# Sixteen-head attention in a four-layer kernel: value products with the probabilities as stationary side

## The chip, the cores and the metric

The kernel runs on one core of a Trainium2 chip. The metric is the device time of one execution in microseconds (us). The engines are named as in the profile: PE is TensorE's matmul, PEld its load of the stationary operand, DVE is VectorE, ACT ScalarE, POOL GpSimd, SP SyncE.

## The reference

The program has four layers. Each adds a cross attention between 512 positions of x (four batches, width 128) and a context of 77 positions, and then a mixture of experts. The change touches the attentions of layers 0, 1 and 2, which have 16 heads of 8 dimensions. Layer 0's, cut:

```python
q = split_heads(queries @ Wq + bq)      # (b, 16, 512, 8)
k = split_heads(keys @ Wk + bk)         # (b, 16, 77, 8)
v = split_heads(values @ Wv + bv)
scores = jnp.einsum('bhqd,bhkd->bhqk', q, k) / jnp.sqrt(jnp.float32(HD))
scores = jnp.where(mask, jnp.float32(-1000000000000000.0), scores)
attn = jax.nn.softmax(scores, axis=-1)
ctx = jnp.einsum('bhqk,bhkd->bhqd', attn, v)
ctx = ctx.transpose(0, 2, 1, 3).reshape(b, sq, d)
return ctx @ Wo + bo
```

Layers 1 and 2 are alike with another mask; layer 1 has no output projection. Layer 3's attention has 8 heads of 128 dimensions and other code. Everything is in float32.

## The kernel before

The three sixteen-head attentions are called stages 0, 1 and 2 here (`attention(l)` in the code). Each is followed by its experts (`feed`). Every engine runs its own program; they meet at semaphores.

A stage goes through four batches of 512 queries. The 16 heads are split into two halves of 8 (index p). The 8 x 77 = 616 rows (head, key) of a half are cut into five pieces of up to 128 rows (`PIECES`), so there are 40 units u a stage (4 batches, 2 halves, 5 pieces), 120 in all. The order is a list of numbered slots n, written out by hand in `attention_plan`: in slot n each engine does the items of that slot, in the order of its own loop, and the PE's loop also does `turned(n - 8)` and `values(n - 10)`. Slot numbers below are counted within a batch, modulo 10.

For each unit, PE forms the scores with (head, key) on the partitions and 512 queries as columns (`turned`: a mask product in bf16, L2198, and a key product, L2200 to L2203); ACT takes the exponential into one of four buffers `pT` (L1190); PE then multiplies by the values (`values`, L2219). The value operand `vx` is block-shaped: for a row of head h it holds the 8 values of that head and a 1 in the head's 9 columns (VC = 9), zeros in the other heads' columns, 72 columns for 8 heads. It is the stationary side; the 512 queries of `pT` move. The five pieces of a half add up in PSUM bank 4 + p, as 72 partitions (8 sums and one denominator for each head) by 512 queries. `pv_done` counts the units.

Then, for each half of a batch (24 in all):

1. ACT copies the 72 x 512 sums to `act_out` (`copy_sums`, L1204, item "O");
2. PE turns them in four blocks of 128 queries back into the same bank, 128 queries on the partitions (`turn_sums`, L2227, item "B", one slot later);
3. DVE divides by the denominators into `onorm` (`norm`, L1703 to L1709, one slot after "B"), waiting on `o_ps`, the count of turns.

In stages 0 and 2 PE then turns `onorm` (`turn_out`, L2235, item "o", slot 3 of the next batch), ACT copies it, PE projects it (`project`, L2242, item "j", slot 4), and DVE adds to x and takes statistics (`update`, L1721 and L1724), from which POOL normalizes x for what follows (L880 to L913). PE turns the normalized x (`turn_x`, L2008), and in stages 0 and 2 forms routing logits (L2041, L2042), which DVE ranks (L1488 to L1526). In stage 1 `update` takes `onorm` directly.

Beside this runs the preparation of the next batch: row scores (`scores`, L2174 and L2175, slots 0 to 7) whose maxima DVE takes (`row_tops`, L1685) and splits (`split_tops`, slot 7), which PE turns (`turn_tops`, L2182, slot 8) and ACT copies; query products (slot 3); and the spread of the values onto the pieces (`spread_values`, L2148, slot 4, and `spread_last_values`, L2155, slot 5), which DVE writes into `vx` (L1669).

The last half's "B" of a stage stands in the experts' code, at their step 0 (`head_plan`), with "o" and "j" at steps 1 and 2. `act_out` is also the experts' buffer in layer 1, so ACT's `func` waits there for all turns (`first`).

Of the kernel before, what the change touches and what calls it, by code (L numbers as in the profile page):

```python
# [58 lines left out]
def build(nc, x_in, ctx_t, ctx_rows, mask0, mask1, mask2, attn_w, cols, rows, gates,  # L59
# [8 lines left out]
    with stack:  # L68
# [3 lines left out]
        def sem(name):  # L72
            return stack.enter_context(nc.semaphore(name))
# [176 lines left out]
        def parts_of(tensor, at):  # L250
# [61 lines left out]
        top_ready, tops_before = gate_done, 1  # L312
        top_ps, turns_before = v_ps, 3
        top_in = sem("top_in")
        t_ready, pv_done, o_ps = sem("t_ready"), sem("pv_done"), sem("o_ps")
        o_used, ont_ready, ot_done, out_ready, x_upd = (
            sem("o_used"), sem("ont_ready"), sem("ot_done"), sem("out_ready"), sem("x_upd"))
        cmv_ready, med_ready, med_ps, med_f, med_hi, med_lo = (
# [8 lines left out]
        xwT_ps, xwT_done, ab_ps, ab_hi, ab_lo, cols_ps, cols_done = (  # L327
            sem("xwT_ps"), sem("xwT_done"), sem("ab_ps"), sem("ab_hi"), sem("ab_lo"), sem("cols_ps"),
            sem("cols_done"))
        ov_done, sums_before = xwT_done, 6  # L330
        mask_ps, mask_in, masks_before = sem("mask_ps"), wq_hi, 1
        xg_ready = sem("xg_ready")
        slots_zero = sem("slots_zero")
# [124 lines left out]
        def attention_plan(l):  # L458
            f = FFNS[l]
            plan = {}  # L460
            for b in range(B):
                at = PRO + UB * b
                if l == 0:
                    if b:
                        place(plan, 6 * b - 2 - (b == 3), ("k", b))
                for s in range(PRO):
                    place(plan, at - UB + s if b else s, ("S", PRO * b + s))
                place(plan, at - UB + 7 if b else 7, ("H", b))
                place(plan, at - UB + 8 if b else 7, ("M", b))
                if b:  # L470
                    place(plan, at - 2 * UB + 3 if b > 1 else 2 - min(l, 1), ("q", b))
                place(plan, at - UB + 4 if b else 5, ("v", b))
                place(plan, at - UB + 5 if b else 6, ("w", b))
                for p in range(NP):
                    place(plan, at + NPC * (p + 1) + 1, ("O", NP * b + p))
                    if (b, p) != (B - 1, NP - 1):
                        place(plan, at + NPC * (p + 1) + 2, ("B", NP * b + p))
                if b < B - 1 and l != 1:
                    place(plan, at + UB + 3, ("o", b))
                    place(plan, at + UB + 4, ("j", b))  # L480
                if b < B - 1:
                    x_at = at + 2 * UB - (2 if b == 2 else 0)
                    place(plan, x_at, ("x", b))
                    if f.route is not None:
                        place(plan, x_at + 2, ("l", b))
                        if b < 2:
                            place(plan, x_at + 6, ("c", b))
            if l == 0:
                place(plan, 18, ("m", 0))
            return plan  # L490
# [588 lines left out]
        def _(act):  # L1079
# [95 lines left out]
            def attention(l):  # L1175
                f, lo = FFNS[l], lo_of(l)

                def softmax(u):
                    i = u % NPC
                    act.wait_ge(t_ready, UL * l + u + 1)  # L1180
                    if u >= 4:
                        act.wait_ge(pv_done, UL * l + u - 3)
                    elif u == 0 and l == 0:
                        act.wait_ge(mask_done, 2)
                    elif u == 0 and l == 1:
                        act.wait_ge(F0.y_used, F0.NS)
                    elif u == 0:
                        act.wait_ge(w3_stored, 32 * NE)
                    r = slice(0, PIECES[i][1])
                    a.activation(pT[u % 4][r, :], bank(2 + u % 2)[r, :], ACT.Exp).then_inc(p_ready, 1)  # L1190

                def copy_tops(b):
                    act.wait_ge(top_ps, turns_before + B * l + b + 1)
                    for p in range(NP):
                        a.activation(qst(l, b)[96:P, 2 * p:2 * p + 2, :], bcast(bank(6)[96:P, :], 2, 1), ACT.Copy
                                     ).then_inc(top_in, 1)

                def copy_sums(bp):
                    b, p = bp // NP, bp % NP
                    act.wait_ge(pv_done, UL * l + UB * b + NPC * (p + 1))  # L1200
                    if b:
                        act.wait_ge(o_ps, NP * (B * l + b - 1) + p + 1)
                    r = slice(0, PH * VC)
                    a.activation(act_out[p][r, :], bank(4 + p)[r, :], ACT.Copy).then_inc(ov_done, 1)  # L1204

                def copy_oT(b):
                    act.wait_ge(ont_ready, B * lo + b + 1)
                    a.activation(oT, bank(7), ACT.Copy).then_inc(ot_done, 1)

                for n in range(NATT + 2):  # L1210
                    what, b = LEFT_AT[l].get(n, ("", 0))
                    if what == "x":
                        x_high(2 * l, b, bank(7))
                    elif what in ("ab", "vo"):
                        wide_weights(b, int(what == "vo"), bank(7))
                    elif what == "turn":
                        weights_turned(1, b, bank(7))
                    elif what == "cols":
                        wide_cols()
                    for what, b in APLAN[l].get(n - 1, []):  # L1220
                        if what == "c":
                            route_copy(f, b, bank(6))
                    if PRO <= n < PRO + UL:
                        softmax(n - PRO)
                    for what, b in APLAN[l].get(n - 2, []):
                        if what == "l":
                            route_exp(f, b)
                    for what, b in APLAN[l].get(n, []):
                        if what == "x":
                            x_high(f.index, b, bank(6))  # L1230
                        elif what == "q":
                            q_high(l, b, bank(6))
                        elif what == "M":
                            copy_tops(b)
                        elif what == "O":
                            copy_sums(b)
                        elif what == "o":
                            copy_oT(b)
                        elif what == "k":
                            copy_mask(l, b, bank(6))  # L1240
                    if l == 0 and n == 20:
                        act.wait_ge(med_f, 1)
                        a.activation(xh[:].rearrange("p (b k) -> p b k", b=B)[:, :, S:KEYS],
                                     med[:].rearrange("p (b k) -> p b k", b=B), ACT.Copy).then_inc(med_hi, 1)
                return copy_oT

            def feed(f, copy_oT):
                l = f.nth

                def first(k):  # L1250

                    if f is F1 and k < 2:
                        act.wait_ge(o_ps, NP * B * 2)

                def func(k):
                    act.wait_ge(f.g_ready, k + 1)
                    if f.gated:
                        first(k)
                        if k >= 2:
                            act.wait_ge(f.hf_done, k - 1)  # L1260
                        ins = a.activation(act_out[k % 2][:], bank(f.g_banks[k % 2]), f.func)  # L1261
# [165 lines left out]
        def _(dve):  # L1427
# [232 lines left out]
            def attention(l):  # L1660
# [34 lines left out]

                def norm(bp):
                    b, p = bp // NP, bp % NP
                    dve.wait_ge(o_ps, NP * B * l + bp + 1)
                    if l or bp:
                        dve.wait_ge(o_used, NP * B * l + bp)  # L1700
                    o4 = bank(4 + p)[:, 0:TB * PH * VC].rearrange("p (t h c) -> p t h c", t=TB, h=PH)
# [277 lines left out]
        def _(pe):  # L1979
# [161 lines left out]
            def attention(l):  # L2141
# [64 lines left out]
                def values(u):  # L2206
                    b, p, i = u // UB, u // NPC % NP, u % NPC
                    pe.wait_ge(p_ready, UL * l + u + 1)
                    if i == 0:
# [6 lines left out]
                        else:  # L2216
                            pe.wait_ge(FFNS[l - 1].y_used, FFNS[l - 1].NS)
                    r = slice(0, PIECES[i][1])
                    mm(bank(4 + p)[0:PH * VC, :], vx[b % 2][r, i, p, :, :].rearrange("r h c -> r (h c)"), pT[u % 4][r, :],  # L2219
                       start=(i == 0), stop=(i == NPC - 1)).then_inc(pv_done, 1)  # L2220

                def turn_sums(bp):
                    p = bp % NP
                    pe.wait_ge(ov_done, sums_before + NP * B * l + bp + 1)
                    r, w = slice(0, PH * VC), PH * VC
                    for t in range(TB):
                        ins = nc.tensor.transpose(bank(4 + p)[:, t * w:(t + 1) * w], act_out[p][r, t * P:(t + 1) * P],  # L2227
                                                  ident[r, r])
                    ins.then_inc(o_ps, 1)

                def turn_out(b):
                    dst = use7(ot_done, B * lo + b + 1)
# [18 lines left out]
                for n in range(NATT):  # L2251
# [22 lines left out]
                    if n >= PRO + 2:  # L2274
                        values(n - PRO - 2)
                    for what, b in items:
                        if what == "B":
                            turn_sums(b)
                        elif what == "o":
                            turn_out(b)  # L2280
                        elif what == "j":
                            project(b)
# [14 lines left out]
                        elif what == "m":  # L2297
# [3 lines left out]
                                ins = nc.tensor.transpose(dst[:, c * KC:(c + 1) * KC], crow[:, c, :],  # L2301
                                                          ident[0:KC, 0:KC])
                            ins.then_inc(med_ps, 1)
                return turn_sums, turn_out, project

            def feed(f, tail):
                l = f.nth
# [55 lines left out]
                for k in range(f.end):  # L2363
# [2 lines left out]
                    if k >= LAG:  # L2366
                        down(k - LAG)
                    for what, b in f.head.get(k, []):
                        turn_sums, turn_out, project = tail
                        if what == "B":  # L2370
                            turn_sums(b)
                        elif what == "o":
                            turn_out(b)
                        elif what == "j":
                            project(b)
# [257 lines left out]
```

## Time and profile before

| | |
|---|---|
| median of 3 runs | 1604.9 us (1604.57 to 1605.0) |
| the profiled execution | 1607.48 us |
| its span in the trace | 1605.7 us |
| mean granted PE clock | 0.931 of full speed |
| busy, share of the span | PE 88%, PEld 69%, DVE 64%, ACT 53%, POOL 34% |

Busy time is the sum of the times in which an engine has an instruction under way. An f32 product is recorded as two passes, each with its own load. A granted clock of 1.00 is 2.4 GHz, one of 0.50 is 1.2 GHz. Records of PE are latencies and overlap; how close together they can stand is seen in the chain, where a merged piece "x8" has the time from the first to the last.

### The profile page before, as it was taken

The page shows a single profiled execution, that of the slowest core. Times are in us where ns is not written, and L with a number is a line of the kernel's source. Part 1 is how long each engine was busy: PE and PEld are TensorE (multiplying, and loading weights), DVE is VectorE, ACT ScalarE, POOL GpSimd, SP SyncE. Part 2 cuts the span into 40 slices and gives each one's busy share as a digit, 9 for nine tenths or more (in the row PEclk, how much of TensorE's full clock was granted, in tenths as well). Part 3 has the DMA queues.
Part 4 walks back from the last instruction along what each step waited for, and adds up shares of the span by engine and source line. Part 5 has one row for each costly group of instructions (what it writes and reads, how often), then busy time and mean ns, then how long its engine had stood idle before and what let it go on. Part 6 is the DMA issues. An engine that isn't in the chain of part 4 may idle for free.

```text
span 1605.7 us, 22012 instructions
## 1 busy us (share of the span) xinstructions
PE 1407.7 (88%) x7236; PEld 1113.6 (69%) x7236; DVE 1029.3 (64%) x2075; ACT 847.1 (53%) x1607; POOL 543.5 (34%) x880
## 2 busy tenths in 40 slices
PE   3899799799999999988899998779999989875992
PEld 3655567555788888755578886568878878765992
DVE  4445578744666666755467776567776877745773
ACT  1244566335555555433577775456655656533661
POOL 7632511512332233341212102242323343332674
PEclk7699899799999999989999999789999999986996
DMA  6130232120913333311033000120000000033963
GB/s 151 32 91 2 60 112 92 40 61 19 251 40 106 131 118 109 109 40 60 11 70 119 29 25 1 50 108 1 1 5 12 1 15 1 20 153 100 382 255 86
DMA packets 67791, 123.14 MB, mean 77 GB/s; under 512 B 10200, under 2 KB 43792, under 8 KB 66399
## 3 DMA queue, kind: packets, MB, share of 16 engines
q1 hardware_dynamic: 40495, 104.57, 19.7%
q10 hardware_dynamic: 24688, 12.70, 3.0%
q0 software_dynamic: 2496, 4.47, 0.8%
q8 instruction: 59, 0.97, 0.2%
q14 instruction: 53, 0.43, 0.1%
HBM read 82.61 MB, written 29.16 MB: 70 GB/s over the span
## 4 chain that ended last, share of the span: by engine, by line
PE 67%; DVE 12%; POOL 8%; issue 8%; DMA 2%; ACT 2%; ACTq 0%; POOLq 0%; SPq 0%; DVEq 0%
PE psum L1983 11%; PE psum L1985 11%; PE psum L1984 11%; PE psum L2219 5%; PE psum L2359 4%; PE psum L2360 4%; PE psum L2361 4%; PE psum L2454 3%; PE psum L2174 2%; PE psum L2175 2%; POOL y_dram L994 2%; PE psum L2198 1%; POOL slots_dram L963 1%; PE psum L2203 1%; PE psum L2008 1%
## 5 line engine op out<-in xcount | busy, mean ns | idle before, releaser
L1798 DVE TENSOR_TENSOR hhl<-psum,hhl 128x512 fp32r<-128x512 f32 x336 | 230.3, 686 | 85.0 <-ACT hhl L1273 82.9
L1273 ACT ACTIVATE hhl<-psum 128x512 fp32r<-128x512 f32 x336 | 199.4, 594 | 3.4 <-DVE psum L1794 3.2
L1983 PE MATMUL psum<-xh,wl 128*128 128x512 f32 x464 | 190.2, 410 | 3.2 <-DVE hhl L1798 2.5
L1984 PE MATMUL psum<-xl,wh 128*128 128x512 f32 x464 | 185.4, 400 | 0.0
L1985 PE MATMUL psum<-xh,wh 128*128 128x512 f32 x464 | 184.7, 398 | 0.0
L1062 POOL TENSOR_SCALAR shared<-shared,xrd 128x589 f32<-128x589 f32 x128 | 97.4, 762 | 234.7 <-DVE xrd L1886 234.3
L1263 ACT ACTIVATE psum<-psum 128x512 f32<-128x512 f32 x208 | 120.9, 582 | 72.3 <-PE psum L1985 71.0
L1345 ACT ACTIVATE hhl<-psum 128x512 fp32r<-128x512 f32 (+1 forms) x160 | 95.3, 596 | 117.6 <-PE psum L2454 116.3
L1685 DVE TENSOR_REDUCE topneg<-psum 128x8 f32<-128x616 f32 x96 | 76.3, 797 | 118.1 <-PE psum L2175 117.6
L2359 PE MATMUL psum<-hhl,wl 128*128 128x512 f32 x336 | 135.5, 403 | 12.8 <-DVE xn L1818 9.4
L1794 DVE TENSOR_TENSOR psum<-act_out,psum 128x512 f32<-128x512 f32 x128 | 89.0, 695 | 85.6 <-PE psum L1985 79.9
L1891 DVE TENSOR_TENSOR hhl<-psum,hhl 128x512 fp32r<-128x512 f32 (+1 forms) x160 | 110.2, 689 | 50.0 <-ACT hhl L1345 48.8
L1261 ACT ACTIVATE act_out<-psum 128x512 f32<-128x512 f32 x128 | 76.5, 598 | 122.6 <-PE psum L1985 122.2
L2360 PE MATMUL psum<-hhl,wh 128*128 128x512 f32 x336 | 133.8, 398 | 0.0
L2361 PE MATMUL psum<-hhl,wh 128*128 128x512 f32 x336 | 133.8, 398 | 0.0
L880 POOL TENSOR_SCALAR vpe<-mv 128x4 f32<-128x4 f32 x32 | 8.1, 254 | 367.0 <-DVE mv L1437 366.4
L1190 ACT ACTIVATE shared<-psum 128x512 f32<-128x512 f32 (+1 forms) x120 | 70.6, 596 | 111.6 <-PE psum L2203 98.4
L2219 PE MATMUL psum<-shared,late 128*72 128x512 f32 (+1 forms) x240 | 126.3, 611 | 0.0
L943 POOL TENSOR_SCALAR wh<-late 128x1024 fp32r<-128x1024 f32 (+2 forms) x25 | 26.4, 1057 | 284.4 <-PE psum L2361 257.9
L2454 PE MATMUL psum<-ident,shared 128*128 128x128 f32 (+1 forms) x640 | 98.7, 278 | 8.5 <-POOL shared L1062 8.4
L1983 PEld LDWEIGHTS psum<-xh,wl 128*128 128x128 f32 x464 | 88.8, 191 | 24.3 <-DVE hhl L1798 3.0
L1337 ACT ACTIVATE shared<-psum,xnm 128x589 f32<-128x589 f32 x128 | 95.9, 749 | 17.9 <-DVE xnm L1880 16.2
(399 smaller groups left out, 3659.1 us busy)
## 6 DMA issues: line engine op xcount, KB each, us to landing
w3late<-w_dram SPq DMA_DIRECT2D x24, 768.0 KB
abkb<-w_dram SPq DMA_DIRECT2D x18, 768.0 KB
w_dram<-shared SPq DMA_DIRECT2D x16, 768.0 KB, 5.8
shared<-comb_dram SPq DMA_DIRECT2D x10, 1024.0 KB, 4.6
slots_dram<-late ACTq DMA_DIRECT2D x1, 9792.0 KB, 36.7
shared<-comb_dram SPq DMA_DIRECT2D x24, 256.0 KB
late<-in_f_dram SPq DMA_DIRECT2D x8, 768.0 KB, 5.5
shared<-in_f_dram SPq DMA_DIRECT2D x8, 768.0 KB, 7.4
```

Source lines behind the costliest of these rows:

```text
L1263: ins = a.activation(h_bank(f, k), h_bank(f, k), f.func)
L1273: a.activation(hh[k % 4], h_bank(f, k), ACT.Copy).then_inc(f.hh_done, 1)
L1798: v.tensor_tensor(hl[k % 4], h_bank(f, k), hh[k % 4].bitcast(f32), ALU.subtract).then_inc(f.h_ready, 1)
L1891: v.tensor_tensor(hl[k % 4][r, :], bank(5 + k % 2)[r, :], hh[k % 4][r, :].bitcast(f32), ALU.subtract).then_inc(xt_lo, 1)
L1983: mm(dst, ll, rh, start=start, stop=False)
L1984: mm(dst, lh, rl, start=False, stop=False)
L1985: return mm(dst, lh, rh, start=False, stop=stop)
L2219: mm(bank(4 + p)[0:PH * VC, :], vx[b % 2][r, i, p, :, :].rearrange("r h c -> r (h c)"), pT[u % 4][r, :], start=(i == 0), stop=(i == NPC - ...
L2359: mm(dst, lo[:, o:o + P], hh[k % 4], start=(c == 0), stop=False)
L2360: mm(dst, hi[:, o:o + P], hl[k % 4], start=False, stop=False)
L2361: mm(dst, hi[:, o:o + P], hh[k % 4], start=False, stop=(c == f.nf - 1)).then_inc(f.h_used, 1)
L2454: ins = nc.tensor.transpose(bank(5 + k % 2)[r, qt * P:(qt + 1) * P], xprob[(4 * u + qt) % XS][:, j * P:j * P + r.stop], ident[:])
```

## The change

The value product changes sides. For a unit, each of four blocks of 128 queries of `pT` is the stationary operand, and the 72 columns of `vx` move. The result lands with 128 queries on the partitions, in the same layout that the turns used to leave (`bank(4 + p)`, 72 columns for each block of queries). The copy of the sums, their turn and the semaphores `o_ps` and `ov_done` go. `norm` waits on `pv_done`, and "B", which now concerns DVE alone, stands one slot earlier except for the last half of a stage. The guard `first` in the experts of layer 1 goes.

```diff
                 for p in range(NP):
-                    place(plan, at + NPC * (p + 1) + 1, ("O", NP * b + p))
                     if (b, p) != (B - 1, NP - 1):
-                        place(plan, at + NPC * (p + 1) + 2, ("B", NP * b + p))
+                        place(plan, at + NPC * (p + 1) + 1, ("B", NP * b + p))
...
-                def copy_sums(bp):
-                    b, p = bp // NP, bp % NP
-                    act.wait_ge(pv_done, UL * l + UB * b + NPC * (p + 1))
-                    if b:
-                        act.wait_ge(o_ps, NP * (B * l + b - 1) + p + 1)
-                    r = slice(0, PH * VC)
-                    a.activation(act_out[p][r, :], bank(4 + p)[r, :], ACT.Copy).then_inc(ov_done, 1)
...
-                def first(k):
-
-                    if f is F1 and k < 2:
-                        act.wait_ge(o_ps, NP * B * 2)
...
                 def norm(bp):
                     b, p = bp // NP, bp % NP
-                    dve.wait_ge(o_ps, NP * B * l + bp + 1)
+                    dve.wait_ge(pv_done, UL * l + UB * b + NPC * (p + 1))
...
                     r = slice(0, PIECES[i][1])
-                    mm(bank(4 + p)[0:PH * VC, :], vx[b % 2][r, i, p, :, :].rearrange("r h c -> r (h c)"), pT[u % 4][r, :],
-                       start=(i == 0), stop=(i == NPC - 1)).then_inc(pv_done, 1)
-
-                def turn_sums(bp):
-                    p = bp % NP
-                    pe.wait_ge(ov_done, sums_before + NP * B * l + bp + 1)
-                    r, w = slice(0, PH * VC), PH * VC
+                    w = PH * VC
                     for t in range(TB):
-                        ins = nc.tensor.transpose(bank(4 + p)[:, t * w:(t + 1) * w], act_out[p][r, t * P:(t + 1) * P],
-                                                  ident[r, r])
-                    ins.then_inc(o_ps, 1)
+                        ins = mm(bank(4 + p)[:, t * w:(t + 1) * w], pT[u % 4][r, t * P:(t + 1) * P],
+                                 vx[b % 2][r, i, p, :, :].rearrange("r h c -> r (h c)"),
+                                 start=(i == 0 and t == 0), stop=(i == NPC - 1 and t == TB - 1))
+                    ins.then_inc(pv_done, 1)
```

The rest of the diff removes the names `o_ps`, `ov_done` and `turn_sums` and the calls of the removed functions.

## Rows read from the trace of the kernel before

**Rows 1.** The page: busy us (share of the span) and instructions.
```profile
PE 1407.7 (88%) x7236; PEld 1113.6 (69%) x7236; DVE 1029.3 (64%) x2075; ACT 847.1 (53%) x1607; POOL 543.5 (34%) x880
```

**Rows 2.** Windows: the attentions. Length, busy PE, PEld, DVE, ACT, POOL, PEclk, DMA, GB/s.
```profile
69.10:170.00 100.90, 93.83 (x459) 57.08 (x457) 47.38 (x127) 42.21 (x74) 30.34 (x68) 0.95 0.14 37
318.00:400.00 82.00, 79.32 (x342) 44.09 (x341) 38.57 (x92) 36.43 (x58) 12.91 (x27) 0.96 0.13 39
707.00:794.60 87.60, 80.57 (x388) 47.29 (x386) 40.95 (x111) 36.89 (x61) 12.91 (x27) 0.98 0.13 37
sum 270.50, PE 253.72 PEld 148.46 DVE 126.90 ACT 115.53 POOL 56.16; mean PE 84.57 PEld 49.49 DVE 42.30 ACT 38.51 POOL 18.72
```

**Rows 3.** The chain that ended last, stage 0: start us, us, what.
```profile
114.06 0.25 PE psum L2227 x4
...
114.76 0.86 PE psum L2219 x2
```

**Rows 4.** Source lines L2219 and L2242, loads: ns min/median/max, first and last start.
```profile
L2219 PEld LDWEIGHTS psum<-shared,late x240: 140/143/244, 68.8 to 794.2; 128*72 128x72 f32 x96, 104*72 104x72 f32 x24
...
L2242 PEld LDWEIGHTS psum<-late,tops x64: 187/192/333, 103.2 to 801.1; 128*128 128x128 f32 x64
```

**Rows 5.** The chain: passes with one (L2099, L2108) and 128 (L2242) moving columns.
```profile
77.73 0.79 PE psum L2099 x8
78.52 1.79 PE psum L2108 x16
...
103.75 0.89 PE psum L2242 x8
```

**Rows 6.** Source lines L1204 and L2227, the copy and the turn of the sums.
```profile
L1204 ACT ACTIVATE act_out<-psum x24: 592/593/595, 85.6 to 795.2; 72x512 f32<-72x512 f32 x24
...
L2227 PE MATMUL psum<-ident,act_out x96: 223/226/284, 88.3 to 796.1; 72*128 72x72 f32 x96
```

**Rows 7.** Timeline, turn_out on PE: start, us, what, and in brackets the idle before.
```profile
100.55 0.63 PE L2235 MATMUL psum<-ident,shared 128*128 128x128 f32 x4 [0.40 <-DVE shared L1709]
...
173.72 0.96 PE L2235 MATMUL psum<-ident,shared 128*128 128x128 f32 x4 [2.40 <-DVE shared L1709]
```

**Rows 8.** Timeline, stage 0, third batch's end: logits, norm, ranks, turn of x.
```profile
150.56 0.25 PE L2042 MATMUL psum<-ghl,xl 128*128 128x8 f32 x1
...
151.19 0.36 DVE L1703 RECIPROCAL rden<-psum 128x32 f32<-128x32 f32 x1 [2.64 <-PE psum L2227]
...
151.92 0.18 DVE L1488 COPY logits<-psum 128x32 f32<-128x32 f32 x1
...
163.24 0.73 PE L2008 MATMUL psum<-ident,xn 128*128 128x128 f32 x4 [1.98 <-POOL xn L913]
```

**Rows 9.** Timeline, end of stage 1, ACT.
```profile
402.52 1.28 ACT L1261 ACT_TABLE_LOAD   x1 [1.08 <-PE psum L2227]
```

**Rows 10.** Windows: stretches before and after the clock's falls. Columns as in rows 2.
```profile
76.00:82.00 6.00, 6.00 (x46) 5.12 (x44) 1.93 (x5) 0.99 (x4) 0.00 (x0) 0.98 0.04 9
78.50:80.30 1.80, 1.80 (x19) 1.80 (x19) 0.73 (x3) 0.00 (x0) 0.00 (x0) 1.00 0.00 0
81.80:85.10 3.30, 3.30 (x11) 1.97 (x10) 0.99 (x2) 0.60 (x1) 0.00 (x0) 0.50 0.44 107
...
132.50:136.00 3.50, 1.36 (x7) 0.42 (x5) 2.89 (x12) 0.60 (x1) 1.00 (x3) 1.00 0.01 2
136.40:139.70 3.30, 3.30 (x9) 1.33 (x8) 1.00 (x2) 0.98 (x2) 2.82 (x7) 0.50 0.00 0
...
163.70:167.00 3.30, 3.30 (x7) 1.31 (x6) 0.69 (x1) 1.19 (x2) 2.30 (x8) 0.50 0.00 0
...
351.40:354.70 3.30, 3.30 (x9) 1.71 (x8) 1.46 (x3) 0.60 (x1) 1.88 (x2) 0.50 0.41 99
...
764.40:767.70 3.30, 3.30 (x10) 1.42 (x8) 1.00 (x2) 1.19 (x2) 2.86 (x6) 0.50 0.00 0
```

**Rows 11.** Timeline, stage 1, third batch, the spread of the last values.
```profile
376.23 0.49 PE L2155 MATMUL psum<-late 77*128 77x128 f32 x2 [0.25 <-DVE late L1669]
```

More of the change, by code:

```diff
@@ L314, in build @@
         top_in = sem("top_in")
-        t_ready, pv_done, o_ps = sem("t_ready"), sem("pv_done"), sem("o_ps")
+        t_ready, pv_done = sem("t_ready"), sem("pv_done")
         o_used, ont_ready, ot_done, out_ready, x_upd = (
@@ L329, in build @@
             sem("cols_done"))
-        ov_done, sums_before = xwT_done, 6
         mask_ps, mask_in, masks_before = sem("mask_ps"), wq_hi, 1
@@ L1234, in attention @@
                             copy_tops(b)
-                        elif what == "O":
-                            copy_sums(b)
                         elif what == "o":
@@ L1257, in func @@
                     if f.gated:
-                        first(k)
                         if k >= 2:
@@ L2276, in attention @@
                     for what, b in items:
-                        if what == "B":
-                            turn_sums(b)
-                        elif what == "o":
+                        if what == "o":
                             turn_out(b)
@@ L2303, in attention @@
                             ins.then_inc(med_ps, 1)
-                return turn_sums, turn_out, project
+                return turn_out, project
             def feed(f, tail):
@@ L2368, in feed @@
                     for what, b in f.head.get(k, []):
[L2369 to L2372, printed above, removed]
+                        turn_out, project = tail
+                        if what == "o":
                             turn_out(b)
```

## The prediction

> **What bounds the kernel now.** I read the page's busy shares first: PE 88% of the span, DVE 64%, ACT 53% [rows 1]. Then the stretches of the three sixteen-head attentions, the only places that the diff touches: together 270.5 us, in which PE is busy 253.7 us, DVE 126.9 and ACT 115.5 [rows 2]. So here too PE sets the pace, and what leaves ACT is worth only what waits for it. The chain of waits says the same: it runs through PE step by step. The value product of a step is a link of 0.86 us, the turn of the sums one of 0.25 us [rows 3]. Not all of the stages is like that: behind the second and third batches of stages 0 and 2 the chain leaves PE for DVE and POOL (norm, ranks, update, normalization).
>
> **The value steps.** There are 120. Each is now one f32 product of 72 stationary and 512 moving columns, which the trace has as 2 passes (240 records [rows 4]), 0.86 us at full clock [rows 3]. It becomes four products of 128 stationary and 72 moving columns, thus 8 passes. The moving part of a pass shrinks: the sums' turn moves 72 f32 columns in 0.25/4 = 0.06 us [rows 3]. But each pass needs a stationary load of 128 f32 columns, 192 ns where the 72-column one took 143 [rows 4, 5]. What sequences of such loads cost is in the trace: 8 passes with one moving column 0.79 us, 16 with one 1.79, 8 with 128 columns 0.89 [rows 5]. The price of 0.10 to 0.11 us hardly depends on the moving columns up to 128, so the load sets it. New step: 7 x 0.11 + 0.06 to 0.11 for the last = 0.83 to 0.88, middle 0.86. Cost over 120: between -3.6 and +2.4 us; I take +0.5. The moving work in a step falls from all of 0.86 us to 8 x 0.06 = 0.48: the array is without columns for almost half of the step. That is the point of this forecast, below.
>
> [...]
>
> **Copy and turn of the sums.** 24 ACT copies of 593 ns, 14.2 us, go [rows 6]. They lie beside PE's products and only the turn waits for them, so ACT's time itself is worth nothing. Of PE's 24 groups of four turns (226 ns each, overlapping, 0.25 us a group [rows 3, 6]) I count 20: the last group of stages 0 and 2 stands before a wait of PE for DVE (2.40 us in stage 0, alike in stage 2) that stays [rows 7], since DVE is then busy with the ranks, and the group before it is followed by the wait for POOL. 20 x 0.25 = -5.0 us.
>
> **Norm one slot earlier.** DVE's norm (0.7 us from its start to that of the next work [rows 8]) waited for the turn; it now follows the value products directly and stands one slot earlier, so turn_out finds it done. In slot 3 of the second and third batches of stages 0 and 2 PE waited for it, 0.40 us in the one shown, alike in the other three [rows 7]: 4 x 0.40 = -1.6. In slot 3 of the fourth batch DVE waited 2.64 us for the turn, then did norm, and only at 151.92 began the ranks, whose logits were ready at 150.81; from there DVE, then POOL, lead to the PE wait of 1.98 us at 163.24 [rows 8]. In stages 0 and 2: 2 x 1.1 = -2.2. What is late next there is POOL, unchanged. At the end of stage 1, ACT waited 1.08 us for the last turn before it could load the table for the experts' function [rows 9]; that guard is gone, and DVE and PE waited behind it: -1.0. Against it: in slot 7 norm now stands ahead of the split of the row tops on DVE, for which the turn of the tops in PE's slot 8 waits. Between them PE has a slot's products, of which the value step alone is 0.86 us; I take 0.1 us for each of three batches in stage 1, where norm is longer by a factor, and 0 elsewhere: +0.3. No DMA moves.
>
> Without the clock: +0.5 - 5.0 - 1.6 - 2.2 - 1.0 + 0.3 = -9.0 us.
>
> **The clock.** Five times in these stages the granted clock falls from 2.4 to 1.2 GHz: at 81.7, 136.4, 163.7, 351.4 and 764.4 us. Before the last four PE was idle for a good part (1.36 us busy of 3.5 before the second; the others are alike). Before the first it was not: 6.00 us busy of 6.00, and 1.80 of them consisted of stationary loads with one-column products [rows 5, 10]. So loads did not keep the clock, although PE's records show no gap. After each fall PE did mask, key, full value products and turns without a gap and the clock was back within about 3.4 us; each fall cost some 1.7 us. The new value steps are half-way to that stretch of one-column products: 0.48 of 0.86 us with columns, and as they take most of a slot, I expect that the clock comes back much later, at places where PE has long runs of other products: turn_out with queries, and project with the spread of values (at 103.75 [rows 5]), once a batch at best, or at the experts. [...]
>
> Price: from the falls to those places are 103.7 - 81.7 = 22, 170 - 136.4 = 34 (with the fall at 163.7), 376 - 351.4 = 25 [rows 11] and 794.6 - 764.4 = 30 us: 111, less 5 x 3.4 already low = 94, of which PE is busy 94% [rows 2]: 88 us of work that would take twice as long, +88. The other bound is that it returns as before, 0. Row tops, blocks of x and scores give shorter full runs on the way, so I take 41% of the way: +36. Nearer to the middle than to 0, because a stretch with a wait of PE that kept its clock may also lose it now, when the steps around the wait are half-filled.
>
> Profiled execution: 1607.5 - 9.0 + 36 = 1634.5 (its span is 1605.7; the median of the runs, 1604.9, is 2.6 below its time): 1632.
>
> **Rivals.** (1) The clock behaves as before. For it: PE is never idle in a step. Against: the row at 78.5. Time 1604.9 - 9 = 1596, by the step's bounds 1592 to 1599. This is the case of the other side; it decides if the stretch after each fall is as short as now. (2) The loads hide and a pass costs its columns, 0.06 us as in the turn, whose loads have 128 columns too: step 0.50, 120 x 0.36 = -43 more, 1553. Against: all three rows of loads. (3) The clock is low through most of the stages: half of the 253.7 us of PE work at half clock would be +127, less 9 and less the waits of DVE that a slower PE swallows: about 1710. (4) The clock costs only some 9 us, falls that last one short stretch longer, and cancels the gain: 1602 to 1608.
>
> **Chances.** Forecast (clock late, +15 to +84): 0.60, its own range 1611 to 1680. (1) 0.25, (2) 0.03, (3) 0.07, (4) 0.05. Slower 0.67, faster 0.28, same (within 0.2%, 3.2 us, about what a measurement of this kernel can tell) 0.05. The range 1592 to 1680 takes in (1), (4) and all but the edges of the forecast; it leaves out (2) and (3).
>
> **What would show it.** The value step's records: 960 loads of 192 ns, 8 passes in 0.83 to 0.88 us at full clock. If a step is 0.5 to 0.7, (2) holds. The row of granted clock: long runs near 0.5 in the stages of rows 2. If the stages' mean clock stays at 0.95 to 0.98 as in rows 2, the forecast is wrong and (1) holds. PE should not wait for norm in slot 3; the waits for POOL should be there still, shorter where PE is slow. ACT's share falls by 14 us. The experts' stretches and the wide attention should keep their durations. The likeliest error is the size of the clock's term: it depends on where the falls come to lie against the long runs.

## The result, and the profile after

The changed kernel takes 1620.55 us (median of 4 runs, 1619.11 to 1626.61), the kernel before 1604.74 us beside it (4 runs, 1603.97 to 1605.0): ratio 1.0103, 95% interval 1.0084 to 1.0123, so 16 us slower. The profiled execution took 1620.65 us, with a span of 1618.9 against 1605.7. Forecast was 1632 us, within 1592 to 1680. Medians are of all runs; one execution each of two versions below, of 1610.34 and 1631.51 us, counts as slow and is left out of the ranges given there.

The page of the changed kernel, busy us and the row of granted clock (40 slices of 40.5 us):
```profile
PE 1425.4 (88%) x7860; PEld 1209.6 (75%) x7860; DVE 1027.8 (63%) x2075; ACT 834.2 (52%) x1583; POOL 544.9 (34%) x880
...
PEclk7777889889999999987899999979999999996996
```
ACT gave up 12.9 us [rows 1] and DVE 1.5, and the kernel is slower: they were not the bound. PE is 17.7 us busier.

The attentions, from the first value product to the start of the last one of each stage (windows; length, busy of PE, PEld, DVE, ACT, POOL, PEclk), first the kernel before, cut in this way:
```profile
69.00:168.80 99.80, 92.73 (x455) 56.61 (x454) 46.31 (x122) 41.75 (x72) 30.37 (x69) 0.95 0.14 38
320.90:400.20 79.30, 76.62 (x333) 42.17 (x332) 36.96 (x89) 35.24 (x56) 12.91 (x27) 0.98 0.14 41
703.30:794.60 91.30, 84.27 (x402) 49.28 (x400) 41.84 (x113) 38.14 (x63) 12.91 (x27) 0.98 0.12 36
```
and then the changed one:
```profile
67.80:182.10 114.30, 108.47 (x668) 97.18 (x666) 45.87 (x127) 37.73 (x66) 30.75 (x70) 0.79 0.12 33
333.20:410.20 77.00, 74.12 (x546) 65.82 (x544) 36.72 (x90) 32.38 (x50) 12.96 (x27) 1.00 0.16 46
709.00:812.10 103.10, 97.05 (x614) 85.97 (x613) 41.71 (x114) 34.12 (x56) 12.96 (x27) 0.83 0.11 32
```
Read two columns, the length and PEclk. Stage 0 is 14.5 us longer and stage 2 11.8, stage 1 is 2.3 shorter: together 270.4 became 294.4, +24.0. In the two long stages the mean clock is 0.79 and 0.83 instead of 0.95 and 0.98; in stage 1 it is 1.00. The clock records of these traces are all 1.00 or 0.50, so a clock of 0.79 over 114.3 us is 0.21 x 2 x 114.3 = 48 us at half speed; all three stages together have 83 us of it, before 17. A microsecond at half clock does about half a microsecond's work (a new step takes 1.61 us there and 0.84 at full clock, as shown below), so 66 us more of it cost 33. What is left of the +24 is -9, the size of the forecast's terms without the clock. (The second decimal of PEclk leaves this open by about 2 us; the raw clock records have 81.4 us at half clock in these windows and 17.1 before, so 32 instead of 33.)

The new steps, in the chain: two in a row at full clock with the scores between them, and one at half clock.
```profile
350.91 0.84 PE psum L2203 x8
351.75 0.19 PE psum L2156
351.94 0.15 PE psum L2157
...
352.83 0.84 PE psum L2203 x8
```
```profile
89.01 1.61 PE psum L2203 x8
```
The same slots in the kernel before:
```profile
338.77 0.86 PE psum L2219 x2
339.63 0.14 PE psum L2174
339.76 0.15 PE psum L2175
...
340.66 0.86 PE psum L2219 x2
```
A step is 0.84 us, 0.02 less than before. But the first score product behind it takes 0.19 instead of 0.14 (it will be 0.18, 0.16 and 0.14 with 88, 104 and 128 moving columns below). That its load hides less well behind a short pass fits this row of numbers; it is a reading, not a measurement. So a slot with scores is 1.92 us instead of 1.89 (352.83 - 350.91, 340.66 - 338.77), and the 120 steps together cost about what they did: 0.02 less on each, 0.05 more on what follows, which in the chain is so behind some two in five of them.

The source lines of the steps, loads and products:
```profile
L2203 PEld LDWEIGHTS psum<-late,shared x960: 187/192/338, 67.6 to 812.0; 128*128 128x128 f32 x168, 104*128 104x128 f32 x24
L2203 PE MATMUL psum<-late,shared x960: 223/275/467, 67.8 to 812.1; 128*128 128x72 f32 x168, 104*128 104x72 f32 x24
```

What PE waited for, us in total, times and the longest, in stage 0 and then in stage 2:
```profile
PE psum L2137 <- DVE late L1651: 4.3, 2, 2.2
PE psum L1990 <- POOL xn L911: 1.5, 1, 1.5
```
```profile
PE psum L2137 <- DVE late L1651: 4.5, 3, 2.1
PE psum L1990 <- POOL xn L911: 1.3, 1, 1.3
```
The waits of 0.40 us for norm ahead of turn_out [rows 7] are gone. The long ones are those of the spread of the last values (spread_last_values, L2137) for DVE, about 2.15 us twice in each of these stages. The kernel before has them too, of the same length, four in all, as its row for stage 0 shows:
```profile
PE psum L2155 <- DVE late L1669: 4.3, 2, 2.1
```
At the end of these waits lie the clock's falls. Windows: the stretch with the first such wait, the stretch that follows it at half clock, the next one after 145.10, and in stage 2 after 742.40 and 776.60:
```profile
107.50:111.00 3.50, 1.35 (x12) 1.16 (x11) 3.10 (x12) 0.60 (x1) 0.80 (x3) 0.99 0.46 111
111.00:131.40 20.40, 20.40 (x82) 17.45 (x82) 4.69 (x10) 5.72 (x9) 6.32 (x17) 0.50 0.17 52
...
145.10:155.30 10.20, 9.97 (x39) 8.23 (x39) 2.99 (x8) 1.78 (x3) 6.79 (x18) 0.50 0.01 2
...
742.40:762.90 20.50, 20.48 (x80) 17.54 (x81) 4.28 (x9) 5.51 (x8) 3.83 (x7) 0.50 0.29 96
...
776.60:790.30 13.70, 13.27 (x53) 11.29 (x53) 3.19 (x9) 3.12 (x5) 4.14 (x9) 0.50 0.01 1
```
Compare with [rows 10]: after its falls in the stages the kernel before was back within 3.4 us. Here PE is busy for all of 20.40 us, with a record at every moment, and the clock stays at 0.50. No row has the clock in GHz. What the trace of the kernel before shows, in the chain through the first experts: products of 512 moving columns follow each other every 0.43 us at a clock of 0.50 (205.78 to 207.91), 1.2 columns a ns, and every 0.23 us at 1.00 (228.05 to 229.43), 2.2 a ns. Taken as one column a cycle, the first makes 1.2 GHz, and its double is 2.4: an estimate, not a row. The fall at 80.2 us, behind the products with one column, has no wait before it and lasts 10.2 us.

### The profile page after: what moved, and what is told of

The parts are those of the page before. It is cut to its first block, busy times and chain, and to the rows that moved or that the text cites. A ratio compares the mean times of both kernels' runs of the same rounds, so it can differ in the third digit from the quotient of the medians.

```text
span 1618.9 us, 23216 instructions
## 1 busy us (share of the span) xinstructions
PE 1425.4 (88%) x7860; PEld 1209.6 (75%) x7860; DVE 1027.8 (63%) x2075; ACT 834.2 (52%) x1583; POOL 544.9 (34%) x880
## 4 chain that ended last, share of the span: by engine, by line
PE 69%; DVE 12%; POOL 8%; issue 6%; DMA 2%; ACT 2%; ACTq 0%; POOLq 0%; DVEq 0%; SPq 0%
PE psum L1965 11%; PE psum L1967 11%; PE psum L1966 11%; PE psum L2203 6%; PE psum L2334 4%; PE psum L2335 4%; PE psum L2336 4%; PE psum L2427 3%; PE psum L2156 2%; PE psum L2157 2%; PE psum L2180 2%; POOL y_dram L992 2%; POOL slots_dram L961 2%; PE psum L2185 1%; PE psum L1990 1%
## 5 line engine op out<-in xcount | busy, mean ns | idle before, releaser
L2203 PEld LDWEIGHTS psum<-late,shared 128*128 128x128 f32 (+1 forms) x960 | 144.1, 216 | 11.3
L2203 PE MATMUL psum<-late,shared 128*128 128x72 f32 (+1 forms) x960 | 137.5, 293 | 0.0
L1967 PEld LDWEIGHTS psum<-xh,wh 128*128 128x128 f32 x464 | 88.8, 191 | 21.6
```

The source lines that it names most:

```text
L1967: return mm(dst, lh, rh, start=False, stop=stop)
L2203: ins = mm(bank(4 + p)[:, t * w:(t + 1) * w], pT[u % 4][r, t * P:(t + 1) * P], vx[b % 2][r, i, p, :, :].rearrange("r h c -> r (h c)"), sta ...
```

## The experiments

Two theories stood against each other. A: the value steps with 72 moving columns are what keeps the clock low after a fall. B: the new steps cost more in themselves, or the new order of the work does.

**More moving columns for the same work.** The two halves' values of a piece lie side by side (144 columns). The product may move 128, 104 or 88 of them instead of its own 72; the surplus sums land in unused PSUM columns, and norm reads past them. The number of products and loads is that of the changed kernel.
```
+            both = vx[b % 2][r, i, :, :, :].rearrange("r p h c -> r (p h c)")
+            side = both[:, 0:VW] if p == 0 else both[:, 2 * PH * VC - VW:2 * PH * VC]
-            ins = mm(bank(4 + p)[:, t * w:(t + 1) * w], pT..., vx[b % 2][r, i, p, ...],
+            ins = mm(bank(4 + p)[:, t * VW:(t + 1) * VW], pT..., side,
```
128 columns:

> The changed kernel, but the moving side of each value product is 128 columns of the two halves' values instead of 72 (56 columns of the result are not read). Theory A (the clock comes back late because the 8 passes of a step leave the array without columns for almost half of it): a pass still costs about 0.11 us, a step 0.89 instead of 0.84, +5 us in all, but the low stretches in the three attentions shrink from 75 us (five stretches of 10 to 20) to about 17 (3.4 each): 1620.5 + 5 - 29 = about 1597. Theory B (stationary loads of the probabilities or waits make it slower, the clock is a by-product): time stays at 1620 or rises by the 5 us, 1620 to 1626.

Measured 1590.21 us (1587.36 to 1593.04, 6 runs), the kernel before 1606.44: ratio 0.9909 (0.9886 to 0.9931). Stages 0 and 2, and a step:
```profile
64.80:162.20 97.40, 91.92 (x667) 82.95 (x666) 45.29 (x123) 37.52 (x65) 30.51 (x70) 0.95 0.14 39
...
689.00:779.90 90.90, 85.23 (x615) 76.17 (x613) 41.74 (x115) 33.99 (x56) 12.91 (x27) 0.96 0.13 36
```
```profile
93.00 0.89 PE psum L2207 x8
93.89 0.14 PE psum L2159
```
Each step does more and costs 0.05 us more, of which the score product behind it gives 0.05 back (0.14 instead of 0.19), and the kernel is 30 us faster than with 72 columns. Its waits for DVE are as long as before (4.2 us, two, in stage 0), and the clock still falls at two of the four; what differs is how soon it is back (6.8 us both times). B can't give that sign.

104 columns:

> As e1_wide128 with 104 moving columns: columns fill 0.087 of a pass of 0.11 us. Theory A: between the changed kernel and e1_wide128, with low stretches of 20 to 50 us in the attentions, 1598 to 1612. Theory B: 1620 to 1624, as the changed kernel.

Measured 1590.86 us (4 runs), ratio 0.9912 (0.9884 to 0.9941), a step 0.87 us.

88 columns:

> As e1_wide128 with 88 moving columns: columns fill 0.073 of a pass of 0.11 us. Theory A: nearer to the changed kernel than e2_wide104, 1605 to 1621. Theory B: 1620 to 1622.

Measured 1606.83 us (1600.84 to 1613.77, 10 runs), ratio 1.0004 (0.9985 to 1.0024), a step 0.86 us. The stages, 0 to 2, of its profiled execution (1611.01 us, 4 above the median):
```profile
66.20:177.70 111.50, 105.79 (x668) 94.51 (x667) 45.84 (x124) 37.63 (x65) 30.53 (x69) 0.82 0.13 34
328.30:405.50 77.20, 74.40 (x546) 66.06 (x544) 36.68 (x90) 32.37 (x50) 12.91 (x27) 1.00 0.15 46
704.20:797.90 93.70, 87.77 (x614) 78.68 (x612) 41.72 (x115) 34.10 (x56) 12.92 (x27) 0.93 0.12 35
```
With 72, 88, 104 and 128 columns the stages hold 83, 53, 17 and 17 us at half clock (worked out from PEclk as above; the raw clock records have 81, 55, 17 and 18) and take 294.4, 282.4, 265.3 and 266.5 us. The price of a step at full clock rises by 0.05 us on the way, so the clock decides. Behind a wait of PE it was back after 10.2 to 20.5 us in the changed kernel and with 88 columns, after 3.4 to 6.8 with 104 and 128. Each of these traces is one execution.

**The one-column products of the kernel before.** The forecast rested on the fall at 81.7, where PE had been full of loads with one-column products [rows 10]. Here the kernel before does 12 of those products with the column repeated 128 times; the surplus is written over or not read:
```
-                query_columns(1, dst)
+                for e in range(4):
+                    mm(dst[:, 4 + e:132 + e], xwT[...], xc[:, 4 + e:5 + e].broadcast_to([P, P]), ...)
```


> The kernel before, with the 12 one-column products of the bias columns (24 passes, 2.6 us) at 79 us widened to 128 moving columns by repeating the column. Theory A: loads with one column do not hold the clock, loads with 128 do, at the same 0.11 us a pass; the fall at 81.7 us vanishes and with it some 1.7 us: 1603. Theory B (PE's clock there falls for another reason): the fall stays, 1604.7.

Measured 1608.62 us (12 runs), ratio 1.0012 (0.9996 to 1.0028). In its chain the products take 0.89 and 1.79 us, where they took 0.79 and 1.79 ([rows 5]), and in the window with them and what follows the clock is whole:
```profile
80.75 0.89 PE psum L2106 x8
81.64 1.79 PE psum L2110 x16
```
```profile
80.50:85.10 4.60, 4.60 (x36) 3.89 (x36) 1.63 (x4) 0.93 (x3) 0.00 (x0) 1.00 0.05 13
```
So the reading of that row was right: PE was busy throughout in both versions, for nearly the same time; the clock fell behind the products with one column and not behind those with 128. It won no time. In the profiled execution the clock fell at other places instead (stage 0 has 0.93, stage 2 0.95): behind all four waits of 2.14 us, where the kernel before lost it behind two, and three of its six falls in the stages lasted 6.8 us. So with the old value steps too the clock isn't always back within 3.4 us; stretches of 10 us and more behind a wait are found in the stages with 72 and 88 columns only. The busy row alone doesn't tell here which clock is granted: it is full in both versions (6.00 of 6.00 us, 4.60 of 4.60).

**Norm in its old slot, with 128 columns.**
```
-                        place(plan, at + NPC * (p + 1) + 1, ("B", NP * b + p))
+                        place(plan, at + NPC * (p + 1) + 2, ("B", NP * b + p))
```


> The version of e1_wide128 with norm (item B) back in its old slot. If the slot is worth what the prediction said (PE's wait in slot 3 four times 0.4 us, and the ranks' start twice 1.1 us), it is 3.8 us slower than e1_wide128, less what the removed copy and turn save of it anyway: +2 to +4 us. Rival: the gain came from the removed copy and turn alone, and the slot is worth nothing: the same as e1_wide128.

Measured 1595.78 us (6 runs), ratio 0.9931 (0.9912 to 0.9949) against 0.9909 with the new slot. The ratios are 3.5 us apart, and the intervals overlap. That looks like the forecast's 3.8 us, but the traces don't bear it out. PE waits for norm ahead of turn_out again (0.7 us in stage 0, 0.7 in stage 2), and the stages take 268.1 us instead of 266.5 at the same time at half clock (17.4 and 17.6 us): 1.6 us, the forecast's term for the waits. PE's wait for POOL, in which the other 2.2 us should show, is 1.3 us in stage 0 and 1.1 in stage 2 in both versions. The rest of the difference lies outside the stages, where this execution has 6.7 us more at half clock.

This version also shows what the slot does in stage 1. With the new slot PE waits there for the tops' negation (1.5 us in all, longest 1.1) and hardly for the low part of the queries (0.4); with the old one it is 0.5 and 1.5 (longest 1.3), as in the kernel before, and the clock's fall behind that wait is back too (at 345.8, for 3.4 us).

**Fillers where PE waits.** The changed kernel, and ahead of the spread of the last values in the third and fourth batch of stages 0 and 2 PE does 20 bf16 products of 224 columns whose sums nobody reads:
```
+                    if l != 1 and b >= 2:
+                        for j in range(20):
+                            mm(bank(4)[:, 288:512], maskT[:, mask_slot(l, b), 0:P], spreadb[:, 0:224], ...)
```


> The changed kernel (72 moving columns) with 20 bf16 products of 224 columns, not read by anyone, on PE where it waits for spread_last_values in the third and fourth batches of stages 0 and 2 (1.9 of 2.1 us). Theory A (a fall needs a wait of PE or one-column products; the half-filled steps only delay the return): the four falls at such waits vanish, the low stretches in the attentions shrink from 75 to 10 to 25 us, 1595 to 1603. Rival (the half-filled steps lose the clock by themselves): falls come elsewhere, 1612 to 1622.

Measured 1590.41 us (1585.97 to 1592.9, 8 runs), ratio 0.9912 (0.9881 to 0.9944). The timeline of PE at the first of the places, and the windows of stages 0 and 2, from the fastest of the runs (1585.97 us):
```profile
105.19 2.09 PE L2137 MATMUL psum<-late 77*128 77x224 bf16 x20
107.49 0.49 PE L2141 MATMUL psum<-late 77*128 77x128 f32 x2 [0.22 <-DVE late L1651]
```
```profile
64.60:163.90 99.30, 97.33 (x708) 88.64 (x706) 45.85 (x127) 37.53 (x66) 30.79 (x70) 0.92 0.14 38
...
688.50:777.70 89.20, 87.00 (x653) 78.74 (x652) 42.27 (x117) 34.44 (x58) 12.95 (x27) 0.97 0.13 37
```
The wait of 2.15 us became 0.22 behind 2.09 us of fillers, so DVE delivers no sooner, and all four falls at these waits are gone, with the 72 columns kept. 30 us came back for work that PE does for nobody. Of the falls that remain, that behind the one-column products lasts 10.2 us (at 76.8) and that behind the first wait for POOL 13.7 (at 158.7), both as in the changed kernel; a new one, behind the second wait for POOL, lasts 6.8 (at 773.1). So two things come together: something takes the clock, here a wait of PE or the one-column products, and the half-filled steps then keep it away. Without the one, as here, or without the other, as with 128 columns, about 30 us are back.

The same with 104 columns (24 fillers of 96 columns, the rest of 512 beside 4 x 104):

> The version of e2_wide104 with 24 products of 96 columns in the same four waits. Theory A: two to three falls of 3.4 to 6.8 us fewer than e2_wide104, each worth 1.7 to 3.4 us: 4 to 8 us faster. Rival: the products delay the next step, which was about to start: same time.

Measured 1588.12 us (4 runs), ratio 0.9876 (0.986 to 0.9892), against 0.9912 (0.9884 to 0.9941) without the fillers: the intervals overlap a little. The stages take 262.2 us instead of 265.3, with 10.2 us at half clock instead of 17.

**Outputs and projection a slot earlier.** turn_out and project of a batch stand one slot earlier in stages 0 and 2:
```
-                    place(plan, at + UB + 3, ("o", b))
-                    place(plan, at + UB + 4, ("j", b))
+                    place(plan, at + UB + 2, ("o", b))
+                    place(plan, at + UB + 3, ("j", b))
```
With 128 columns:

> The version of e1_wide128 with turn_out and project (items o and j) one slot earlier, since norm is done earlier. If PE's wait for spread_last_values (2.1 us, four times) comes from the update that stands behind project on DVE, it goes down by most of itself, also the stretches that cost the clock: 5 to 12 us less than e1_wide128. Rival: turn_out now waits for norm as before the change and the gain is lost there: same time within 2 us.

Measured 1585.05 us (1582.93 to 1585.68, 5 runs), ratio 0.9854 (0.984 to 0.9867): the fastest version, 22 us under the kernel before beside it (1607.32). The stages take 262.1 us, 4.4 less than with 128 columns alone. But the wait ahead of spread_last_values didn't go down by most of itself in all four places, as expected: in two of them a wait of 2.1 us now stands one item earlier, ahead of spread_values (for the low part of the queries). PE's waits in stages 0 and 2 add up to 8.5 us instead of 11.0, and the time at half clock in the stages went from 17.6 to 10.2.

With the 72 columns of the change:

> The changed kernel with its 72 moving columns as it is, and the turn of the outputs and the projection one slot earlier (stages 0 and 2). With 128 columns this edit gave 5 us (ratio 0.9909 to 0.9854). Theory A (half-filled steps delay the return of the clock after a wait of PE): the waits stay, so the low stretches stay long, and the time is 1612 to 1622, ratio 1.005 to 1.011. Rival (it is the waits' length that sets how often and how long the clock is low, whatever the columns): with shorter waits the time comes near 1595, ratio 0.993.

Measured 1618.78 us (1603.44 to 1626.31, 12 runs; median 1615.39 without the highest), ratio 1.0076 (1.0044 to 1.0107). Stages 0 and 2, of an execution of 1603.57 us, the second fastest:
```profile
65.10:167.00 101.90, 96.69 (x668) 86.92 (x667) 45.44 (x123) 37.56 (x65) 31.05 (x71) 0.90 0.14 37
...
692.20:794.00 101.80, 97.08 (x614) 85.87 (x612) 41.35 (x114) 34.12 (x56) 13.01 (x27) 0.83 0.11 32
```
PE's waits are somewhat shorter (5.2 us instead of 5.8 in stage 0, 4.8 instead of 6.0 in stage 2), two of the long ones having moved as above, and the kernel still loses in stage 2: an edit worth 5 us with 128 columns is worth little here. The runs spread over 23 us, and that is the clock: a fall can cost 5 or 13 us (the raw clock records have stretches of 10.2 and 27.3 us here), and the mean granted clock goes from 0.926 in the fastest run to 0.911 in that of 1626.31, while span times mean clock stays at 1478 to 1485 us in all.

Both together with 104 columns:

> 104 moving columns, fillers of 96 columns in the slots where PE waits, and the turn of the outputs and the projection one slot earlier. If the gains of the two add up (ratio 0.9876 with the fillers, the early placement worth 0.0055), ratio 0.982, about 1578. If both act on the same wait, ratio 0.985 to 0.988: the fillers, which take about the length of the old wait, now lie where PE waits less, and cost time.

Measured 1595.16 us (1590.5 to 1599.22, 6 runs), ratio 0.9945 (0.9925 to 0.9965). Worse than either; the expectation of 0.982 is missed, and that of 0.985 to 0.988 too. Its profiled execution, the fastest, with a span of 1588.0 us, has stages of 262.8 us, as good as with the fillers alone (262.2). The other five lost time to the clock: their mean granted clock is 0.932 to 0.935 instead of 0.936, and span times mean clock is 1486 to 1489 us in all six. In which stretch they lost it no trace shows.

**The guard at the start of the second experts, with 128 columns.** ACT waits again, but for the last-but-one normalization: the edit waits for 15 of 16, where the expectation speaks of the last.
```
+                        if k < 2:
+                            act.wait_ge(o_used, NP * B * 2 - 1)
```


> The version with 128 moving columns, and at the start of the second experts ACT again waits (for the first two parts) until the last normalization of the sixteen-head attention is done, as it waited for the last turn before. Both theories of the clock expect the same steps. If the guard was worth the forecast 1.0 us, this version is 1 us slower than the one without it (1590.2 against 1606.4 of the kernel before, ratio 0.9909, becomes about 0.9915); the stretch of the second experts goes from 298.7 to about 300. If the guard cost nothing, no difference, and the 4 us that the second experts gained have another reason.

Measured 1590.13 us (6 runs), ratio 0.9912 (0.9893 to 0.9932), and the second experts take 298.7 us, as without it: no difference. The table is loaded at 390.24, before the last value product. So a wait that is over in time costs nothing there. The old guard, which hung on the last turn, isn't restored by this version, and no run measures its price by itself.

## Why the prediction was right, and where it was off

The direction, slower at 0.67, and the reason given for it held. The range alone says little: from 1592 to 1680 it takes in a kernel that is 13 us faster as well.

**Value steps (+0.5): right.** Step 0.84, forecast 0.83 to 0.88, 960 loads of 192 ns. The forecast took almost none of the gain of 0.02 and missed the 0.05 us on the product behind; as that is so behind some two in five steps, both nearly cancel. The rival of hidden loads is out. A pass took 0.84/8 = 105 ns with 72 moving columns, 0.89/8 = 111 with 128. Faster passes with loads of 128 f32 columns are in the kernel before all the same, those that the rival took as its measure: the turns of the sums are four such loads and four products in 0.25 us [rows 3, 6], 0.06 each, with loads of 141 ns instead of 192 (source L2227). Why the turns' loads are shorter no run shows, but the value steps went the way of the products in [rows 5], not of the turns.

**Turns of sums (-5.0), waits for norm (-1.6), ranks earlier (-2.2).** The turns and the four waits of 0.40 are gone from the chain. The ranks' term is the one that was mis-sized: PE's waits for POOL are 1.3 and 1.1 us with 128 columns, where PE is at full clock for most of the time as before, instead of 2.0 and 1.5, so 1.1 us and not 2.2, and the version with the old slot has the same 1.3 and 1.1, so it isn't the slot that gave them. With the 72 columns they are 1.5 and 1.3. Together with the steps and the tops these terms make -8.0 within the stages; the windows leave -9.

**Guard (-1.0): too small.** Before, the second experts' stretch (400.20 to 703.30) took 303.1 us, now 298.8 (410.20 to 709.00). The raw clock records have 3.5 us less at half clock in it, worth 1.7, and the cut at the last pass favours the new kernel by some 0.3; about 2.3 are left. (Part of the 1.7 may hang on the guard as well, as the fall in question, at 409.4, comes 5 us behind the wait for ACT; not shown.) ACT now loads its table under the last value steps:
```profile
408.55 1.28 ACT L1243 ACT_TABLE_LOAD   x1
```
Before, the load began at 402.52 [rows 9], and PE, already in the second experts, stood still for ACT's result, as this row of the kernel before shows:
```profile
404.55 0.47 PE L1983 MATMUL psum<-xh,wl 128*128 128x512 f32 x1 [0.68 <-ACT act_out L1261]
```
The forecast counted the 1.08 us of ACT and not what hangs on the whole chain of copy, turn, table load and first result; the split of the 2.3 us among them is not shown.

**Row tops (+0.3): the wait too small, and at another place.** In stage 1 PE waited 1.6 us for the tops' negation (topneg), before 0.5, ahead of the next row scores and not of the turn of the tops. But its wait for the low part of the queries, 1.39 us at 349.79, shrank to 0.25, so the sum of its waits hardly moved (2.6 and 2.9 us). The version with norm in its old slot has the old pair of waits again, so it is norm's new slot that exchanged one for the other. And with the old wait went the fall of the clock at 351.4.

**The clock (+36): the mechanism right, its places half wrong.** In the stages it came to 33. The forecast let each of five falls last 41% of the way to a long run of other products, the one in stage 1 too. That one didn't come at all. The other four came, and two more: stages 0 and 2 lost the clock at every one of their four waits of 2.15 us, and the kernel before, which has the same four waits, had kept it at the first of them in each stage. In stage 0:
```profile
109.57 0.49 PE L2155 MATMUL psum<-late 77*128 77x128 f32 x2 [2.14 <-DVE late L1669]
```
The forecast had named this as a reason to go towards the middle, without a sum of its own. Two errors of opposite sign made a good total. So the size of the sum is in part luck. How long the clock stays away after each fall (10.2 us after 80.2, 20.4 after 111.0, 10.2 after 145.1, 13.7 after 175.8, 20.5 after 742.4 and 13.7 after 776.6) no row of before could tell, and the guess of 41% was one.

**The sum.** Forecast for the profiled execution was 1634.5, measured 1620.65, 13.9 less. Of that 3 are the clock in the stages, 1 their other terms, 3.3 the second experts (4.3 for 1.0); 6.5 lie in the remaining stretches, whose code is untouched, above all behind the last stage (811.1 before, 806.8 after). The kernel before with repeated columns has that last stretch at 808.6: it varies by some microseconds with where the clock falls there (the raw records have 9.3 us less at half clock behind the last stage than before, which is worth about the whole 4.3), and isn't an effect of the change that could be carried over.

**Rivals.** (1), the clock as before, would have been 1596. It hung on whether a stretch behind a fall is as short as before, as the forecast put it. For the 72-column version it is refuted by the windows; with 104 or 128 columns the stretches stay short, and the kernel takes 1591 and 1590. (3), low throughout, and (4), a cost that cancels the gain, are out; the 88-column version comes to the time of (4), 1607, but its clock costs more than the 9 us of (4): 55 us at half clock instead of 17 is worth 19, in an execution of 1611 us.

## What to carry to other kernels

When a product is turned round so that the wide operand becomes stationary, read the granted clock, not the busy row: here PE's busy share stayed at 88%, although 8 x 72 columns move in a step instead of 2 x 512, and the mean clock went from 0.931 to 0.916. See whether loads set the price of a pass, as they seem to here (0.105 us with 72 moving columns, 0.111 with 128); the moving side was then widened nearly for free: 72 to 128 columns cost 0.05 us a step and gave 30 us back. Look next at what takes the clock away: a wait of 2 us cost 5 to 10 us more through the slow stretch behind it (10.2 to 20.5 us at half clock).

## What the runs showed that was not expected

- PE busy for 20.40 of 20.40 us stayed at a clock of 0.50; behind the same wait, the version with 128 columns was back after 6.8 us:
```profile
104.50:111.30 6.80, 6.61 (x24) 5.30 (x25) 2.19 (x5) 0.60 (x1) 5.98 (x14) 0.50 0.55 159
```
- The same wait of 2.1 us takes the clock in one place and not in another of the same kernel (before: kept at 109.57, lost behind 135.52), and where one fall was taken away, others stood elsewhere: the version with repeated columns had a clock of 0.93 and 0.95 in stages 0 and 2 where the kernel before has 0.95 and 0.98. Whether other executions of either have the same falls no trace shows.
- Work that nobody reads, put into a wait, made the kernel 30 us faster (1590.41 against 1620.55, each beside its own runs of before: 0.9912 and 1.0103).
